# Moving a small chain of index arithmetic forward, and giving one bias addition in some visits from VectorE to TensorE

## The reference

```python
logits = x @ router_w
assignments = jnp.argmax(logits, axis=-1)
weights = take_along_axis(softmax(logits), assignments)
hid = gelu(einsum('nd,edf->nef', x, w1) + b1)        # F = 256
all_out = einsum('nef,efd->ned', hid, w2) + b2       # D = 128
x = x + gb * (all_out[own expert] * weights)
```

## Time and profile before

| what | us |
|---|---|
| median of 3 runs | 603.12 |
| lowest of them | 601.77 |
| the profiled execution | 602.05 |
| its span | 600.2 |
| the end of the first stage to the end of the span (DVE note of the ends at 505.33) | 94.9 |

### The profile page before, as it was taken

One profiled execution on the slowest core, in us unless ns is written; L12 is line 12 of the kernel. 1 busy time (PEld: TensorE's weight loads), 2 busy tenths in 40 slices (PEclk: granted clock), 3 DMA queues, 4 the chain that ended last, 5 costly groups with the idle time before them and its releaser, 6 DMA issues.

```text
span 600.2 us, 12121 instructions
## 1 busy us (share of the span) xinstructions
PE 466.0 (78%) x2531; PEld 263.6 (44%) x2531; DVE 550.7 (92%) x1398; ACT 547.8 (91%) x2339; POOL 486.1 (81%) x647
## 2 busy tenths in 40 slices
PE   5456878887887887787787888778777677999993
PEld 2112433443443343343343343334333345889992
DVE  5899999999999999999999999999999977888994
ACT  2599999999999999999999999999999996678881
POOL 4566777989899988999999898999888687777773
PEclk9555565556556556756655655675665558999997
DMA  6366455544555554545455555666555513798760
GB/s 197 105 192 160 136 139 134 142 140 138 144 141 142 142 149 141 150 143 156 148 155 146 151 146 154 172 177 170 153 150 163 157 64 125 231 335 245 236 198 27
DMA packets 77080, 94.42 MB, mean 157 GB/s; under 512 B 12814, under 2 KB 60718, under 8 KB 77006
## 3 DMA queue, kind: packets, MB, share of 16 engines
q1 hardware_dynamic: 68850, 75.69, 45.7%
q0 software_dynamic: 6144, 16.82, 7.5%
q10 hardware_dynamic: 2015, 1.15, 0.8%
HBM read 58.41 MB, written 35.20 MB: 156 GB/s over the span
## 4 chain that ended last, share of the span: by engine, by line
ACT 44%; POOL 17%; PE 15%; DVE 8%; issue 7%; SPq 3%; DMA 3%; ACTq 1%; POOLq 0%; DVEq 0%
ACT scores L940 43%; PE scores L1263 5%; PE scores L1254 5%; POOL table L847 3%; DVE neg_max L1423 3%; SPq L592 3%; POOL xhat L792 2%; POOL rstd L775 2%; PE scores L1244 1%; POOL rest L581 1%; POOL parts L584 1%; POOL h_scaled L815 1%; DMA x_s<-table 1%; POOL att L804 1%; DMA more_rooms<-table 1%
## 5 line engine op out<-in xcount | busy, mean ns | idle before, releaser
L940 ACT ACTIVATE scores<-scores,neg_max 128x256 f32<-128x256 f32 x1024 | 467.2, 808 | 10.8 <-DVE neg_max L1423 10.6
L940 ACT ACTIVATION_READ_ACCUMULATOR scores<-scores,neg_max 128x1 f32 x1024 | 419.8, 569 | 0.0
L1423 DVE TENSOR_REDUCE neg_max<-scores 128x4 f32<-128x1024 f32 x256 | 309.3, 1211 | 7.4 <-PE scores L1104 6.8
L1104 PE MATMUL scores<-k_stack,q_stack 64*128 64x256 bf16 x1024 | 148.2, 388 | 79.6 <-ACT scores L940 65.5
L1104 PEld LDWEIGHTS scores<-k_stack,q_stack 64*128 64x128 bf16 x1024 | 34.1, 106 | 163.5 <-ACT scores L940 116.2
L847 POOL DMA_INDIRECT table<-rows,place_i x64 | 66.1, 1034 | 20.6 <-issue 15.2
L792 POOL TENSOR_SCALAR xhat<-rows,mv,rstd 128x128 f32<-128x128 f32 x60 | 47.6, 794 | 6.8 <-POOL rstd L775 6.8
L1263 PE MATMUL scores<-w_s,hid 128*128 x308 | 49.2, 284 | 1.4 <-DVE y_biased_s L1993 1.2
L1132 PE MATMUL side_a<-w_gated,opt_t 128*128 128x128 f32 x128 | 49.8, 491 | 0.0
L784 POOL TENSOR_SCALAR xhat<-x_s,mv,rstd 128x128 f32<-128x128 f32 x62 | 49.0, 798 | 0.4 <-POOL rstd L775 0.4
L906 POOL DMA_INDIRECT out_dram<-x_s x40 | 39.2, 980 | 12.2 <-issue 8.8
(11 more groups left out here) (230 smaller groups left out, 882.1 us busy)
## 6 DMA issues: line engine op xcount, KB each, us to landing
q_stack<-parts_dram SPq DMA_DIRECT2D x192, 64.0 KB, 2.9
x_s<-table SPq DMA_DIRECT2D x62, 192.5 KB
parts_dram<-parts SPq DMA_DIRECT2D x31, 384.0 KB
k_stack<-parts_dram SPq DMA_DIRECT2D x186, 64.0 KB, 2.3
mod_b<-mod_rows SPq DMA_DIRECT2D x32, 256.0 KB, 4.4
x_s<-in_x_dram SPq DMA_DIRECT2D x13, 256.0 KB, 5.1
table<-pad_tile SPq DMA_DIRECT2D x15, 192.5 KB
more_rooms<-table SPq DMA_DIRECT2D x15, 192.5 KB
```

The source lines that it names most:

```text
L940: last = act.activation(buf[:, k * L:k * L + L], buf[:, k * L:k * L + L], ACT.Exp, bias=neg_max[:, p, n:n + 1], accum_out=exp_sum[:, p, n: ...
L1104: last = pe.matmul(scores[:, c, at:at + L], q_stack[p][r, g + j, t * P:t * P + P], k_stack[p][r, g + j, :], start=True, stop=True)
L1423: dve.tensor_reduce(to, scores[:, (PAIRS * b.n + i) % RING, :].rearrange("p (e j m) -> p e j m", e=2, j=2), AX_X, ALU.max, negate=True).th ...
```

## The change

1. The map's chain is cut into twelve single steps and put between other DVE work, ahead of the whole of visit 2: the first steps between `own_place`, `note_place` and `weigh_last` of the last batch, the others between the biases, gates and sums of visits 0 and 1. `map_columns` comes before `whole_y(2)`. MAP_TURNED goes from 8 to 7, so PE's `turn_map` and DVE's `take_map` stand one step earlier.
2. SP reads the ten numbers of the ends not before the load of visit 14, but behind that of visit 15.
3. In visits 18 to 30 and 68 to 76 (22 visits) PE adds b2: a third product, ones (1 row x 128) by b2's row (1 x 128), float32, into the same PSUM half as the two of `contract`. DVE drops `bias_y` there, and `gate_y` reads PSUM and frees it (it raises `y_biased`). POOL sets the row of ones once, in batch 0.

```diff
-MAP_TURNED = 8
+PE_BIAS = tuple(range(18, 31)) + tuple(range(NT - 9, NT))
+def bias_by_pe(q):
+    return q in PE_BIAS
+MAP_TURNED = 7
...
+def biased_by_dve(q):
+    return sum(1 for k in range(q + 1) if not bias_by_pe(k))
...
                 whole_rows.extend(load_many(sp, tile_row, EARLY, whole_reload(EARLY), 0, PAD_AT))
-                ends.extend(load_many(sp, end_row, FILLS_FIRST, E - FILLS_FIRST, 0, PAD_AT))
...
                 sp.dma_start(rows_in[j % ROOMS][:, :], table[ds(row, P), :]).then_inc(rows_loaded[s], 16)
+                if j == FILLS_FROM - 1:
+                    ends.extend(load_many(sp, end_row, FILLS_FIRST, E - FILLS_FIRST, 0, PAD_AT))
...
                 if b.n == 0:
+                    pool.memset(ones_row[:, :], 1.0).then_inc(ones_row_set, 1)
...
+                adds_bias = bias_by_pe(n)
                 for f in range(FH):
                     last = pe.matmul(expert_out[n % 2], hid[:, n % BUFS, f, :], w2_s[:, ds(expert_of(n), 1), f, :],
-                                     start=(f == 0), stop=(f == FH - 1))
+                                     start=(f == 0), stop=(f == FH - 1 and not adds_bias))
+                if adds_bias:
+                    last = pe.matmul(expert_out[n % 2], ones_row[:, :],
+                                     b2_s[0:1, ds(expert_of(n), 1), :].rearrange("p o d -> p (o d)"), start=False, stop=True)
...
             def gate_y(n):
+                if bias_by_pe(n):
+                    dve.wait_ge(y_done, n + 1)
+                    dve.tensor_tensor(y_gated_s[:, n % 2, :], expert_out[n % 2], rows_in[n % ROOMS][:, GW:GW + D],
+                                      ALU.mult).then_inc(y_biased, 1)
+                    return
...
             def out_y(n):
-                dve.wait_ge(y_gated, n + 1)
+                if bias_by_pe(n):
+                    dve.wait_ge(y_biased, n + 1)
+                else:
+                    dve.wait_ge(y_gated, biased_by_dve(n))
...
                 note_ends()
+                map_rows_left()
                 own_place(other)
+                map_tiles()
                 note_place(other)
+                map_full()
                 weigh_last()
-                for n in range(FIRST):
-                    bias_y(n)
-                for n in range(FIRST):
-                    gate_y(n)
-                for n in range(FIRST):
-                    out_y(n)
-                map_counts()
+                bias_y(0)
+                bias_y(1)
+                map_spread()
+                gate_y(0)
+                map_below()
+                gate_y(1)
+                map_upto()
+                out_y(0)
+                map_bases()
+                map_from()
+                out_y(1)
+                map_in()
+                map_pick()
+                map_sums()
+                map_columns()
                 whole_y(FIRST)
-                map_rows()
-                map_columns()
                 bias_y(FIRST + 1)
                 gate_y(FIRST + 1)
```

More of the change, by code:

```diff
@@ L344, in build_adaln_attention_moe @@
         scale_a = sb("scale_a", [P, B])
+        ones_row = sb("ones_row", [1, P])
         minus_half = sb("minus_half", [P, 2 * LT])
@@ L553, in build_adaln_attention_moe @@
         y_gated = sem("y_gated")
+        ones_row_set = sem("ones_row_set")
         out_ready = sem("out_ready")
@@ L1330, in _ @@
             over_batches(iteration, drain)
+            pe.wait_ge(ones_row_set, 1)
             over_tiles(tile, PRIMED, AT_W2)
@@ L1846, in load_packed, with map_rows_left @@
                 packed_at.extend(load_many(dve, packed_now, at, n, 0, PACKED - 1))
-            def map_counts():
+            def map_rows_left():
                 dve.wait_ge(counted, GROUPS)
-                steps.then(dve.tensor_tensor(early_i[:, 0, :], next_row[0:NT, :], sums_of[:, 3, :], ALU.subtract))
-                steps.then(dve.tensor_scalar(early_i[:, 1, :], early_i[:, 0, :], P.bit_length() - 1, None, ALU.arith_shift_right))
-                steps.then(dve.tensor_copy(n_full, early_i[:, 1, :]))
-                each = n_full.rearrange("p (o e) -> p o e", o=1).broadcast_to([NT, E, E])
-                steps.then(dve.tensor_tensor(tiles_below[:, :, :], below_it[:, :, :], each, ALU.mult))
-                steps.then(dve.tensor_reduce(n_below, tiles_below[:, :, :], AX_X, ALU.add))
-                step["map"] = steps.did(dve.tensor_tensor(n_upto, n_below, n_full, ALU.add))
@@ L1859, in map_rows @@
[L1859 to L1863, removed]
-                tile = tile_no[:, 1:2].rearrange("p (a o) -> p a o", o=1).broadcast_to([NT, 2, E])
-                steps.then(dve.tensor_tensor(in_expert[:, 0:2, :], tile, early_f[:, 1:3, :], ALU.is_ge))
-                steps.then(dve.tensor_tensor(in_expert[:, 2, :], in_expert[:, 0, :], in_expert[:, 1, :], ALU.subtract))
-                steps.then(dve.tensor_tensor(map_p[:, :, :], in_expert[:, 2:3, :].broadcast_to([NT, 2, E]), sums_of[:, 1:3, :], ALU.mult))
+                step["left"] = steps.did(dve.tensor_tensor(early_i[:, 0, :], next_row[0:NT, :], sums_of[:, 3, :], ALU.subtract))
@@ new lines, in map_tiles, with map_full, map_spread @@
+            def map_tiles():
+                steps.after(step["left"])
+                step["tiles"] = steps.did(dve.tensor_scalar(early_i[:, 1, :], early_i[:, 0, :], P.bit_length() - 1, None,
+                                                            ALU.arith_shift_right))
+            def map_full():
+                steps.after(step["tiles"])
+                step["full"] = steps.did(dve.tensor_copy(n_full, early_i[:, 1, :]))
+            def map_spread():
+                steps.after(step["full"])
+                each = n_full.rearrange("p (o e) -> p o e", o=1).broadcast_to([NT, E, E])
+                step["spread"] = steps.did(dve.tensor_tensor(tiles_below[:, :, :], below_it[:, :, :], each, ALU.mult))
@@ new lines, in map_below, with map_upto, map_bases @@
+            def map_below():
+                steps.after(step["spread"])
+                step["below"] = steps.did(dve.tensor_reduce(n_below, tiles_below[:, :, :], AX_X, ALU.add))
+            def map_upto():
+                steps.after(step["below"])
+                step["upto"] = steps.did(dve.tensor_tensor(n_upto, n_below, n_full, ALU.add))
+            def map_bases():
+                steps.after(step["below"])
+                step["bases"] = steps.did(dve.scalar_tensor_tensor(out=sums_of[:, 2, :], in0=n_below, scalar=-float(P),
+                                                                   in1=sums_of[:, 3, :], op0=ALU.mult, op1=ALU.add))
@@ new lines, in map_from, with map_in, map_pick @@
+            def map_from():
+                steps.after(step["upto"])
+                tile = tile_no[:, 1:2].rearrange("p (a o) -> p a o", o=1).broadcast_to([NT, 2, E])
+                step["from"] = steps.did(dve.tensor_tensor(in_expert[:, 0:2, :], tile, early_f[:, 1:3, :], ALU.is_ge))
+            def map_in():
+                steps.after(step["from"])
+                step["in"] = steps.did(dve.tensor_tensor(in_expert[:, 2, :], in_expert[:, 0, :], in_expert[:, 1, :], ALU.subtract))
+            def map_pick():
+                steps.after(step["bases"])
+                steps.after(step["in"])
+                step["pick"] = steps.did(dve.tensor_tensor(map_p[:, :, :], in_expert[:, 2:3, :].broadcast_to([NT, 2, E]),
+                                                           sums_of[:, 1:3, :], ALU.mult))
@@ L1868, in map_rows, with map_sums @@
+            def map_sums():
+                steps.after(step["pick"])
                 step["map"] = steps.did(dve.tensor_reduce(map_f[:, 0:2], map_p[:, :, :], AX_X, ALU.add))
@@ L2015, in whole_y @@
             def whole_y(n):
-                bias_y(n)
+                if not bias_by_pe(n):
+                    bias_y(n)
                 gate_y(n)
@@ L2040, in tile @@
                 elif n > PRIMED:
-                    if in_range(n):
+                    if in_range(n) and not bias_by_pe(n):
                         bias_y(n)
```

1 line of the change is left out of this document (removed).

## The result

The changed kernel takes 612.55 us (median of 6 runs) where the kernel before takes 602.48 (6 runs). The ratio is 1.0169, with a 95% interval from 1.0153 to 1.0185: +9.2 to +11.1 us, slower, though by less than 2%. The profiled execution took 611.35 us with a span of 609.2, against 602.05 and 600.2; so I compare two traces that differ by 9.0 in the span. One of the six runs of the kernel before took 1474.33 us; the median of the other five is 601.97.

What follows compares the result with a forecast made beforehand. TensorE alone was taken to set the pace, 1.00 us a visit. -0.3 + (13c - 1.3) + (9c - 1.5) = 22c - 3.1, +6.8 us at c = 0.45 on 602.05, gave 608.9, rounded to 609; range 602.5 to 612.5.

Steps and rivals of the forecast that it cites:

- The price c: TensorE's time for one bias product with one row of weights: 0.41 to 0.57 us, taken as 0.45.
- into it +0.10, its two records 0.11 to 0.21 and 0.15 to 0.21, the turn behind it +0.05: Split of one bias product's cost on TensorE by starts, in us, giving 0.41 to 0.57.
- 13c - 1.3: Visits 18 to 30: thirteen bias products cost TensorE, less 1.3 us of stalls absorbed; +4.5 us at 0.45 each.
- 9c - 1.5: Visits 68 to 76: nine bias products, less 1.5 us from stalls and the last bias and gate; +2.55 at 0.45 each.
- Part 1: The map moved forward, with SP's ten reads moved behind visit 15's load: -0.3 us together.
- so visit 14's rows come 2.3 us earlier: SP's first load: an earlier map and ten skipped number reads bring its rows 2.3 us forward.
- which is inside the 2.3: SP's ten reads behind visit 15's load delay fills and visit 16's load by 1.0 us, covered by the 2.3 gained.
- inside its slack: GpSimd's last-batch scatter and all its stores start 0.16 us later, within its about 1.8 us of slack.
- 1.00 a visit behind visit 35: Visits 31 to 67 keep their pace of 1.00 us a visit, unchanged.
- no idle TensorE in the bias visits: Visits 18 to 30: TensorE without idle time, at a pace of about 1.45 us a visit.
- GpSimd not the bound: GpSimd stores without a break to 592.93 but has about 1.8 us of slack, so it doesn't bound the kernel.
- its records alone: Rival: each bias product costs only its two records, 0.22 us, total +1.7 us, so 603.8; chance 0.22.

Runs made afterwards that it cites:

- version with late fills: Against the kernel before: map steps early, no bias on TensorE, all fourteen fills issued with loads of visits 16 to 37; 605.44 us, ratio 1.0048.

## Why the prediction was wrong: two terms too small

The direction, the mechanism (TensorE sets the pace from visit 22 on, so a bias that VectorE adds beside it is free, and on TensorE it is paid) and the places were right. The sum was +6.8; the traces differ by +9.0 in the span, by +9.5 behind attention, and the medians by +10.1. The measured median, 612.55, lies just above the range's upper end of 612.5. By its own steps:

- **The price c, step "That gives c = 0.41 to 0.57. I take 0.45".** This step failed first. c is 0.56, at the upper end of its own interval: 22 x 0.11 = +2.5 us. The cause was right, as the version with 128 rows shows (0.22, and +3.1 instead of +10 us in all). The split by starts was right too: "into it +0.10, its two records 0.11 to 0.21 and 0.15 to 0.21, the turn behind it +0.05" measured 0.09, 0.42 for both records and 0.05. What failed is the choice of 0.45 inside it: both records stand at their upper ends. I chose near the lower end, though the earlier trace rows as they stand give the upper: 0.43 - 0.22 on the way in, 0.15 for the record itself and 0.32 - 0.22 behind it are 0.46 for a product of a single record, and the second record's 0.11 makes 0.57.
- **Visits 18 to 30, "13c - 1.3".** 13 x 0.563 less 5.31 makes 2.0 absorbed, 0.7 more than I had. With the cheap product of 128 rows it is the predicted 1.3. That a longer visit swallows more of VectorE's lateness would fit, but isn't shown: in the eight traces without bias products there, visits 22 to 35 take 15.19 to 15.83, and I subtract the one value of 15.46. This error had the other sign.
- **Visits 68 to 76, "9c - 1.5".** 3.42 = 9 x 0.563 - 1.65. Right within 0.15, the gate and bias of the last visit included; alone the nine cost +3.8 measured.
- **Part 1, "-0.3".** In the trace +0.78, and alone +1.6 [0.7 to 2.5] measured (+0.83 in its trace): the sign was wrong. The map's end (3.64 behind the note of the ends, predicted 3.67), the tile rows 1.2 earlier (predicted 1.3) and the turn in time for it held. What failed is the step from there, "so visit 14's rows come 2.3 us earlier", and "which is inside the 2.3". I asked who waits for the map, not what else SP waits for behind it. In before the scatter landed at 513.61, while the ten reads ran (to 513.81), so the load at 514.18 could come at most 0.4 earlier. It came 0.2 later, as the scatter landed 0.55 later; I had let the scatter start 0.16 later "inside its slack", which was GpSimd's slack and not SP's. And the reads, no longer hidden, cost the loads of visits 16 and 17 1.2. More than one trace says so: in the five traces with the old order the rows land 8.07 to 8.59 behind the note and the first load stands at 8.32 to 8.97; in the four with the full change's map steps ahead of `weigh_last` and the early fills they land at 8.72 to 8.91 and it stands at 8.93 to 9.11. With the reads put back the cost by the ratios is 0.4 instead of 1.6, and with `weigh_last` ahead of the map 0.1; the intervals of neighbours in this row overlap, and those of the first and the last touch (1.0011), so the direction is likely and the steps aren't sized.
- **1.00 a visit behind visit 35, no idle TensorE in the bias visits, GpSimd not the bound**: as predicted.

Term by term: 6.8 + 2.49 (c) - 0.71 (absorbed in 18 to 30) - 0.15 (end) + 1.08 (part 1) = 9.51, the shift of the last gate behind the note of the ends. Less the 0.54 by which attention ended earlier that is the 8.97 on the clock of the trace. The spans differ by 9.0, the profiled executions' times by 9.3, the medians by 10.1. The range's upper end was c at its own upper end (22 x 0.57 - 3.1 = 9.4, so 611.5) and 1 us more for the median; it had no room for a part 1 of the other sign, and that was what it lacked.

Of the rivals, "its records alone" (c = 0.22) is what a product of 128 rows gives, not this one. The Trainium skill (TensorE: Matmul & The Clock Gate, section "Step-by-step: what each phase is for") says that a weight load is pulled ahead of running products when the row groups don't conflict or when it goes to the background weights. The traces agree for 128 rows after 128 rows (the load starts 0.11 ahead, 0.22 a product). With one row between them the load starts with its product and the visit costs 0.34 more, so here the measurement decides.

## What to carry to other kernels

Where one engine sets the pace without a gap, work that another does beside it is free, and moving it over costs its full price; read which engine has the gaps before relieving the other. A bias on TensorE should have as many rows of weights as the products around it: 128 rows of 1/128 cost 0.22 us here, one row of ones 0.56. And when a step is moved forward, list every wait between it and its user, those too that have no row in the trace because something ran over them: here the second wait ended 0.6 us ahead of the load that it holds, so at most about 0.35 could be gained, and the steps put ahead of what it waits for made it end later.

## What the runs showed that I had not expected

- A float32 product with one row of weights between products with 128 costs 0.56 instead of 0.22, about 0.1 for each of its records and on the way in, and 0.05 behind; 128 rows of 1/128 take all of the 0.34 away.
- GpSimd's first scatter of the last batch took 2.04 us in three traces in which three small map steps of VectorE stood around `weigh_last`, and 1.77 in four others; in the five traces with the old order and with the map in one piece it took 1.02 to 1.03, with `weigh_last` ahead of the map 0.96 (and the second 1.33). The cause isn't settled, and the map in one piece was no faster.
- The half-clock stretch of the stage behind attention has one of two lengths, and the order of the kernel doesn't decide which: 6.83 us in the traces of before, after and five versions, 3.41 in the seven others. Its place moves too, from 499.86 (map in one piece) to 523.38 (128 rows, in the wait for visit 17's rows). The version with the last nine products is the kernel before up to visit 68, and its stretch is 3.41 long at 512.91 instead of 6.83 at 504.55; the way to its turn of visit 22 is 1.24 longer (23.58 instead of 22.34). So some tenths between two single traces, and even that 1.24, can be nothing that the order did. In the version with late fills a second stretch of 3.41 appeared (547.45 to 550.86).
